# State space stage of a fused convolution and transformer kernel: decay held in PSUM and scanned in two halves, rows of B broadcast by DMA, convolution folded into a weight, preparation moved from VectorE

## The reference, cut to what matters

```python
xi, z = split(W_in @ xn)                      # 128 x 1024 each
xc = silu(conv_b + sum_k conv_w[:, k] * xi[:, t - 3 + k])      # 4 taps along the positions
dt, B, C = split(W_x @ xc)                    # 4, 16 and 16 rows of 1024
delta = softplus(W_dt @ dt + b_dt)            # 128 x 1024
for each position t and each state n:
    h[d, n] = h[d, n] * exp(-exp(A_log[d, n]) * delta[d, t]) + delta[d, t] * xc[d, t] * B[n, t]
    y[d, t] = sum_n h[d, n] * C[n, t]
out = W_out @ ((y + xc * Dp) * silu(z)) + x
```

## Time and profile before

| | us |
|---|---|
| median of 3 runs | 4073.43 (4072.83 to 4073.93) |
| the profiled execution, its time | 4079.2 |
| its span in the trace | 4077.5 |

### The profile page before, as it was taken

How to read it: one execution, slowest core, us unless ns; L and a number is a source line. 1 busy time by engine, 2 the same in 40 slices (tenths; PEclk the granted TensorE clock), 3 DMA queues, 4 the chain that set the end, 5 groups by cost and what they waited for, 6 DMA issues and landing times. The chain is left out here.

```text
span 4077.5 us, 56384 instructions
## 1 busy us (share of the span) xinstructions
PE 3426.7 (84%) x19376; PEld 1233.0 (30%) x19376; DVE 2982.9 (73%) x3235; ACT 2143.2 (53%) x2331; POOL 2103.6 (52%) x586
## 2 busy tenths in 40 slices
PE   6999999999999999999978996567777777767766
PEld 2333333333333333333322333222222222222222
DVE  5677677676776767767722221489999999999999
ACT  3566566565665656656543332255555554555554
POOL 0556556565565555655660000156665666656665
PEclk7999999999999999999998998778888888888888
DMA  2000000000000000000013111200000000000000
GB/s 93 11 14 17 10 14 17 15 14 14 10 17 15 14 15 12 14 15 14 12 39 111 67 36 54 102 9 8 9 12 8 10 8 8 13 8 10 8 8 8
DMA packets 34702, 90.68 MB, mean 22 GB/s; under 512 B 8304, under 2 KB 9396, under 8 KB 34356
## 3 DMA queue, kind: packets, MB, share of 16 engines
q1 hardware_dynamic: 29396, 70.53, 5.6%
q0 software_dynamic: 5056, 16.83, 1.1%
HBM read 49.03 MB, written 38.27 MB: 21 GB/s over the span
## 5 line engine op out<-in xcount | busy, mean ns | idle before, releaser
L526 DVE TENSOR_REDUCE at_pmax<-at_ring 128x1 f32<-128x512 f32 x2048 | 1305.1, 685 | 511.4 <-PE at_ring L334 510.8
L479 ACT ACTIVATE at_probs<-at_sc 128x1024 f32<-128x1024 f32 x1024 | 992.5, 1021 | 659.6 <-PE at_sc L401 659.5
L1623 POOL TENSOR_TENSOR ss_drive<-ss_du,ss_bsb 128x1024 f32<-128x1024 f32 x261 | 865.2, 3333 | 392.4 <-ACT ss_bsb L1469 312.9
L580 POOL TENSOR_TENSOR at_prob_sums<-at_prob_sums,at_probs 128x2048 f32<-128x2048 f32 x192 | 869.4, 4528 | 109.8 <-ACT at_probs L479 98.7
L398 PE MATMUL at_sc<-at_QT,at_KT 32*128 32x512 f32 x4096 | 848.2, 643 | 21.3 <-issue 20.9
L1560 DVE TENSOR_TENSOR_SCAN ss_state<-ss_decay,ss_drive 128x1024 f32<-128x1024 f32 x259 | 774.7, 2991 | 7.5 <-ACT ss_decay L1476 5.1
L580 POOL TENSOR_TENSOR at_prob_sums<-at_probs 128x2048 f32<-128x2048 f32 x64 | 291.0, 4547 | 789.9 <-ACT at_probs L479 789.9
L1377 PE MATMUL ss_Y<-ss_seen,ss_ident 128*128 128x512 f32 x1032 | 598.3, 710 | 58.7 <-DVE ss_yv L1577 58.7
L410 PE MATMUL at_O<-at_probs,at_V 128*32 128x512 f32 x4096 | 538.9, 610 | 53.0 <-DVE at_att L549 51.8
L1469 ACT ACTIVATE ss_bsb<-ss_B 128x1024 f32<-128x1024 f32 x262 | 268.3, 1024 | 537.1 <-PE ss_B L1359 535.9
L334 PE MATMUL at_ring<-at_KH,at_QH 32*128 32x512 bf16 x2048 | 447.3, 389 | 5.7 <-DVE at_pmax L526 2.9
(11 more groups left out here) (192 smaller groups left out, 2846.2 us busy)
## 6 DMA issues: line engine op xcount, KB each, us to landing
scratch_attn<-at_att SPq DMA_DIRECT2D x64, 256.0 KB, 2.0
fc_att<-scratch_attn SPq DMA_DIRECT2D x32, 512.0 KB, 5.8
at_xn<-scratch_xn SPq DMA_DIRECT2D x32, 256.0 KB, 3.8
ss_xn<-scratch_xm SPq DMA_DIRECT2D x17, 256.0 KB, 3.5
ss_xw<-scratch_xw SPq DMA_DIRECT2D x17, 256.0 KB, 3.4
ln_x<-in_x SPq DMA_DIRECT2D x8, 512.0 KB, 4.8
scratch_xn<-ln_xn POOLq DMA_DIRECT2D x8, 512.0 KB, 3.0
fc_x<-in_x SPq DMA_DIRECT2D x8, 512.0 KB, 7.7
```

The costliest lines, as they stand in the source:

```text
L479: nc.scalar.activation(probs[:, kb, two, :].rearrange("p h q -> p (h q)"), sc[:, two, :].rearrange("p h q -> p (h q)"), ACT.Exp, scale=SCA ...
L526: nc.vector.tensor_reduce(pmax[:, quad // 2, h, quad % 2:quad % 2 + 1], ring[:, unit[3], :], AX_X, ALU.max, negate=True).then_inc(max_done, 1)
L580: nc.gpsimd.tensor_tensor(prob_sums[:, half, :, :], before, probs[:, k, :, :], ALU.add).then_inc(pool_sums, 1)
L1623: nc.gpsimd.tensor_tensor(drive[:, n % DEPTH, :], du[:, par, :], bsb[:, n % DEPTH, :], ALU.mult).then_inc(drive_done, 1)
```

## The change

- `decay` becomes a PSUM tile in place of `Bp`, single, in two halves of 512 positions that lie in different banks. ScalarE makes 32 half tiles an image instead of 16 whole ones, one state ahead; VectorE runs two scans a state, the second beginning with the first one's last column.
- The rows of B: ScalarE copies them once an image from `aux` to `brow`, SyncE writes them to memory (`write_rows`, 16 rows of 4 KB) and reads each back into all 128 partitions (`spread_b`), into eight buffers `bsb`, six states ahead. TensorE's 16 spreads of B and ScalarE's 16 copies are gone.
- The convolution: at the start TensorE and ScalarE make `w_taps`, W_in multiplied by each tap's diagonal. `xn` is loaded twice, the second copy one position further, so that two matmuls with 128 contracted rows do four taps. VectorE's four operations and the `xpad` copy are gone; ScalarE makes `pre` with the bias.
- VectorE loses the high part (now ScalarE), the low part and `delta` (now GpSimd), `xc * Dp` (now a diagonal matmul into `Y`) and the addition of x (now an identity matmul, and ScalarE copies the sum in state 2). It keeps the scans, the product with C, the rest, and one product with the gate.
- Softplus: Abs and Relu both read `aux` directly with the bias.
- SyncE now goes state by state. `load_x` of the next image stands at state 3, behind `between`, which stores the image before once `res_done` says that it is there.

The core of the diff, with all that the prediction speaks of:

```diff
-        xn = sb("ss_xn", [P, S])
+        w_taps = sb("ss_w_taps", [P, 2, DI])
+        diag = sb("ss_diag", [P, KC + 1, P])
+        xn = sb("ss_xn", [P, S + KC - 1])
-        decay = sb("ss_decay", [P, DEPTH, S])
-        bsb = sb("ss_bsb", [P, DEPTH, S])
+        brow = sb("ss_brow", [N, 2, S])
+        bsb = sb("ss_bsb", [P, SLOTS, S])
-        aux, Bp, Cp, Y = ps("ss_aux"), ps("ss_B"), ps("ss_C"), ps("ss_Y")
+        aux, decay, Cp, Y = ps("ss_aux"), ps("ss_decay"), ps("ss_C"), ps("ss_Y")
...
         def _(sp):
+            def load_x(b):
+                load(xn[0:C, KC - 1:], xn_d, b, xn_in)
+                load(xn[C:P, KC - 2:KC - 2 + S], xn_d, b, xn_in)
...
+            def write_rows(b, par):
+                sp.wait_ge(brow_done, b + 1)
+                sp.dma_start(rows_d[par], brow[:, par, :]).then_inc(rows_out, DMA)
+
+            def spread_b(b, par, n):
+                if n == 0:
+                    sp.wait_ge(rows_out, (b + 2) * DMA)
...
+                    sp.wait_ge(drive_done, b * N + n - SLOTS + 1 + DEPTH)
+                sp.dma_start(bsb[:, n % SLOTS, :], rows_d[par, n:n + 1, :].broadcast_to([P, S])).then_inc(b_in[n % SLOTS], DMA)
+
+            def step(b, par, n):
+                if n == AT_REST:
+                    write_rows(b + 1, 1 - par)
+                spread_b(*ahead(b, par, n, B_LEAD))
+                if n == TURN:
+                    sp.wait_ge(gate_done, b + 1)
+                    load_x(b + 1)
+
+            def between(b, par):
+                store(b)
                 load(xw[:, 1 - par, :], xw_d, b + 1, xw_in)
...
+                    for now in loop_steps(2 * j + g, g):
+                        step(*now)
+                    between(2 * j + g, g)
...
         def _(pe):
-            pe.wait_ge(cleared, 3)
+            pe.wait_ge(consts_in, 11 * DMA)
...
+            for k in range(KC):
+                m = nc.tensor.matmul(Cp[0:C, k * DI:(k + 1) * DI], w_plain[:], diag[:, k, :], start=True, stop=True)
...
                     for h in range(2):
-                        m = nc.tensor.matmul(aux[:, hs(h)], w_in[:, 0:DI], xn[:, hs(h)], start=True, stop=True)
+                        for k in range(KC // 2):
+                            m = nc.tensor.matmul(aux[:, hs(h)], w_taps[:, k, :], xn[:, h * HALF + 2 * k:(h + 1) * HALF + 2 * k],
+                                                 start=(k == 0), stop=(k == KC // 2 - 1))
...
                 if n == 0:
-                    pe.wait_ge(y_step, 2 * b + 1)
+                    pe.wait_ge(y_step, b + 1)
+                    for h in range(2):
+                        nc.tensor.matmul(Y[:, hs(h)], diag[:, KC, :], u_in[:, par, hs(h)], start=True, stop=False)
...
             def step(b, par, n):
-                spread_b(*ahead(b, par, n, LEAD + 1))
-
+                if n == 0:
+                    pe.wait_ge(low_done, b + 1)
                 pe.wait_ge(seen_done, b * N + n + 1)
...
                             for h in range(2):
-                                m = nc.tensor.matmul(aux[0:C, hs(h)], w_out[:], yv[1][:, hs(h)], start=True, stop=True)
+                                nc.tensor.matmul(aux[0:C, hs(h)], w_out[:], yv[:, hs(h)], start=True, stop=False)
+                                m = nc.tensor.matmul(aux[0:C, hs(h)], ident[0:C, 0:C], xw[:, g, hs(h)], start=False, stop=True)
                             m.then_inc(out_ready, 1)
...
         def _(act):
+            def take_out(b):
+                act.wait_ge(out_ready, b + 1)
+                act.wait_ge(stored, (b + 1) * DMA)
+                nc.scalar.activation(res[:], aux[0:C, :], ACT.Copy).then_inc(res_done, 1)
...
-                act.wait_ge(state_done, b * N + n + 1)
-                nc.scalar.activation(decay[:, n % DEPTH, :], delta[:, par, :], ACT.Exp, scale=a_neg[:, n:n + 1])\
-                    .then_inc(decay_done, 1)
+                for h in range(2):
+                    if not (isinstance(b, int) and b == 0 and n == 0):
+                        if h == 0:
+                            act.wait_ge(first_half_done, b * N + n)
+                        else:
+                            act.wait_ge(state_done, b * N + n + DEPTH)
+                    nc.scalar.activation(decay[:, hs(h)], delta[:, par, hs(h)], ACT.Exp, scale=a_neg[:, n:n + 1])\
+                        .then_inc(decay_done, 1)
...
-                copy_b(*ahead(b, par, n, LEAD + 1))
-                make_decay(*ahead(b, par, n, LEAD))
+                make_decay(*ahead(b, par, n, 1))
+                if n == 2 and not isinstance(b, int):
+                    take_out(b - 1)
...
         def _(dve):
-                nc.vector.tensor_tensor_scan(state[:, n % 2, :], decay[:, n % DEPTH, :], drive[:, n % DEPTH, :], 0.0,
+                now = state[:, n % 2, :]
+                dve.wait_ge(decay_done, 2 * (b * N + n) + 1)
+                nc.vector.tensor_tensor_scan(now[:, hs(0)], decay[:, hs(0)], drive[:, n % DEPTH, hs(0)], 0.0,
+                                             ALU.mult, ALU.add).then_inc(first_half_done, 1)
+                dve.wait_ge(first_half_done, b * N + n + 1)
+                dve.wait_ge(decay_done, 2 * (b * N + n) + 2)
+                nc.vector.tensor_tensor_scan(now[:, hs(1)], decay[:, hs(1)], drive[:, n % DEPTH, hs(1)], now[:, HALF - 1:HALF],
                                              ALU.mult, ALU.add).then_inc(state_done, 1)
...
-                    nc.vector.tensor_tensor(yv[1][:], yv[0][:], gate[:, par, :], ALU.mult).then_inc(y_step, 1)
+                    nc.vector.tensor_tensor(yv[:], gate[:, par, :], Y[:], ALU.mult).then_inc(y_step, 1)
...
         def _(pool):
+            def low(b, par):
+                pool.wait_ge(mid_done, 2 * b + 2)
+                nc.gpsimd.tensor_tensor(bc[4 * N:6 * N, par, :], bc_rest[:], bc_mid[:], ALU.subtract).then_inc(low_done, 1)
...
             def make_du(b, par):
+                pool.wait_ge(soft_done, b + 1)
+                pool.wait_ge(relu_done, b + 1)
+                nc.gpsimd.tensor_tensor(delta[:, par, :], lin[:], soft[1][:], ALU.add).then_inc(delta_done, 1)
```

More of the change, by code:

```diff
@@ L1218, in state_space_phase @@
     DEPTH = 4
-    assert N % DEPTH == 0
+    SLOTS = 8
+    B_LEAD = 6
+    assert N % DEPTH == 0 and N % SLOTS == 0
     with ExitStack() as ctx:
@@ L1302, in store @@
                 sp.dma_start(out_d[bass.ds(b, 1)].rearrange("a c s -> (a c) s"), res[:]).then_inc(stored, DMA)
-            def image(b, par):
-                sp.wait_ge(gate_done, b + 1)
-                load(xn[0:C, :], xn_d, b + 1, xn_in)
-                if not isinstance(b, int) or b:
-                    store(b - 1)
-                    sp.wait_ge(stored, b * DMA)
-                    sp.sem_inc(res_free, 1)
+            def write_rows(b, par):
+                sp.wait_ge(brow_done, b + 1)
+                sp.dma_start(rows_d[par], brow[:, par, :]).then_inc(rows_out, DMA)
@@ L1313, in image @@
+            def step(b, par, n):
[7 more added lines that the diff above has]
+                store(b)
                 load(xw[:, 1 - par, :], xw_d, b + 1, xw_in)
             load(xw[:, 0, :], xw_d, 0, xw_in)
-            for b in range(2):
-                image(b, b)
@@ L1318, in _ @@
-            with sp.Fori(1, NB // 2) as j:
+            write_rows(0, 0)
+            for n in range(B_LEAD):
+                spread_b(0, 0, n)
+            for n in range(TURN):
+                step(0, 0, n)
+            with sp.Fori(0, NB // 2) as j:
                 for g in range(2):
-                    image(2 * j + g, g)
-            store(NB - 1)
-            sp.wait_ge(stored, NB * DMA)
+                    for now in loop_steps(2 * j + g, g):
+                        step(*now)
+                    between(2 * j + g, g)
@@ L1387, in step @@
                         unit(b + 1, 1 - par, k)
-            for k in range(2):
+            for k in range(4):
                 unit(0, 0, k)
-            pe.wait_ge(consts_in, 11 * DMA)
-            for k in range(2, 4):
-                unit(0, 0, k)
-            for n in range(LEAD + 1):
-                spread_b(0, 0, n)
             for n in range(TURN):
@@ L1447, in softplus @@
                     act.wait_ge(delta_done, b)
[L1448 to L1450 removed]
+                nc.scalar.activation(soft[0][:], aux[:], ACT.Abs, bias=cols[:, 1:2]).then_inc(abs_done, 1)
+                nc.scalar.activation(lin[:], aux[:], ACT.Relu, bias=cols[:, 1:2]).then_inc(relu_done, 1)
                 act.wait_ge(abs_done, b + 1)
@@ L1491, in step @@
                     softplus(b + 1)
-            for n in range(LEAD + 1):
-                copy_b(0, 0, n)
-            for n in range(LEAD):
-                make_decay(0, 0, n)
+            make_decay(0, 0, 0)
             for n in range(TURN):
@@ L1631, in step @@
                 make_drive(*ahead(b, par, n, LEAD))
+            low(0, 0)
             make_du(0, 0)
@@ L1642, in _ @@
                         step(*now)
+                        if now[2] == AT_LOW:
```

(2 more changed lines are left out.)

167 lines of the change are left out of this document (73 added, 94 removed).

## The result

| | before | after |
|---|---|---|
| median, us | 4073.68 (4 runs beside it) | 3974.12 (3961.56 to 3979.77, 4 runs) |
| profiled execution | 4079.2 | 3973.87 |
| its span | 4077.5 | 3972.2 |

The ratio is 0.9751 (95% interval 0.9727 to 0.9774). The change takes 100 us off where 212 were forecast: the sign held, and the time lies in the range of 3780 to 4000, but only in the part that was there for rival (b); the forecast proper, 3820 to 3925, was missed. In the later comparisons the kernel before had a median of 4078.2 (11 runs), 4078.5 (9 runs) and 4075.9 (7 runs), so a difference of 5 us between runs of two comparisons says nothing.

What follows compares the result with a forecast made beforehand. It took VectorE and GpSimd in alternation as the bound; a period of 61.3 + 2.4 + 1.5 + 7.2 = 72.4 us instead of 86.1, with the ends, took 212 off for a median of 3862; range 3780 to 4000.

Steps and rivals of the forecast that it cites:

- (b): More handshakes end late than counted (GpSimd's chain, landings slowed by rows of B, or both): 3925 to 3990 us; chance 0.20.
- the forecast proper: Whole kernel: period 70 to 76 us an image, time 3820 to 3925 us; chance 0.50.
- The scans: VectorE, every state: half scans from PSUM escape the exclusion with GpSimd, at 1.22 and 1.27 us; every drive 2.35.
- The list: VectorE's own work per image: 16 states of 3.69 us, the rest and the gate product, 61.3 us in all.
- The wait at state 4: VectorE waits for TensorE's spread of C, behind the late load of x: 7.2 us an image, bounds 4.7 to 10.7.
- The wait at state 2: VectorE waits for C, spread by TensorE only after four groups of 1.71 us: 1.5 us an image.
- The waits of states 8 to 14: ScalarE's insertions at states 8 and 12 delay the single decay: stalls of 1.3 and 1.1 us, 2.4 an image.
- Ends: Outside first scan to last gate product: start +17 us (8 to 25), end -3.
- (a): The load of x is not late: period 66 us an image, time 3760 us; chance 0.13.
- (c): VectorE's scan still excludes GpSimd's drive: 4040 to 4110 us, near no change; chance 0.04.
- (d): Rows of B, all DMA engines reading the same 4 KB, bound the kernel: 4610 us at a quarter rate; chance 0.13.

Runs made afterwards that it cites:

- e1: Changed kernel with the loads of x issued five states ahead, in state 10, instead of in state 3 behind the store: 3804.54 us.
- e2: Changed kernel with the loads of x issued just ahead of the store of the image before, instead of behind it: 3804.46 us.
- e3: Changed kernel with decay as a single SBUF tile instead of PSUM, still in two halves: 4198.13 us.
- e12: Changed kernel with x five states ahead, output and x products in halves at separate states, and e10's eight filler products: 3755.01 us.
- e9: Changed kernel with 24 bfloat16 filler products on TensorE while it waits for x to land: 3957.53 us.
- e7: Changed kernel with rows of B sent to 16 of 128 partitions from image 1 on (output differs): 3999.33 us.
- e10: e1 with eight filler products in TensorE's idle stretch at the end of state 11: 3799.68 us.

## Why the prediction was wrong in size and right in mechanism

*The step that failed* is the size of VectorE's waits, in the sum 61.3 + 2.4 + 1.5 + 7.2. The forecast had 7.2 at state 4 and 1.5 at state 2 for TensorE's spread of C and 2.4 at states 8 to 14 for ScalarE, 11.1 in all; measured are 16.5, and the wait at state 4 is the largest part of the difference. That the waits at states 2 and 4 would come, and the chain behind them, was right; most of the wait at states 8 to 14 has another cause than the one forecast.

*The scans.* Right. 1.216 and 1.282 against 1.22 and 1.27, drives at 2.35, and without the decay in PSUM the exclusion comes back (4198 and 4103 us). The rate of the Trainium skill (VectorE: DVE Perf Modes, The TRN2 errata) for a source in PSUM, 62 cycles more, does not show: an operation of 1024 columns takes 1.221 with one (the product with C) and 1.218 without (`delta`), and the half scan came out at its price without the addition.

*The list.* 61.3 forecast, 62.9 found. A state takes 3.80 from start to start (3319.57 to 3323.37 in the trace), not 3.69: 0.12 lies between the end of the first half scan and the start of the second, where I took 0.03. The second waits for the first by semaphore, but so does the product with C for the scan before it, and that starts 0.04 behind, so why it is 0.12 stays open. 16 x 0.1 = 1.6.

*The wait at state 4.* This is the term that was mis-sized: 10.3 measured, 7.2 forecast, and within its bounds (4.7 to 10.7) near the worse end. Counted from the end of the gate product (3319.65 in the timeline), link by link: the result is copied at 8.9 (8.3 forecast); the last load is issued at 12.4 (10.45), since the five issues from the store on take 3.5 and not 2.2; it lands at 17.4 (14.65), after 5.0 and not 4.2; C for state 4 is there at 26.2 (22.35), since seven of the eight records of the product are slow, not four. Each link is 0.6 to 1.4 longer, 3.8 together; VectorE wanted it 0.9 later than forecast. The first image and e1 show the term's whole worth, e2 its cause.

*The wait at state 2.* 2.6 in the mean, 1.5 forecast. At the full clock it is 2.12, since the four groups ahead of the spread take 7.6 (3319.80 to 3327.41) and not 4 x 1.71; and it is 3.82 in the quarter of the images in which TensorE is at the half clock, which I had not put there.

*The waits of states 8 to 14.* 3.6 against 2.4. The forecast put them down to ScalarE. That is right only for the 1.0 at state 10 of five images. In the other ten it is C at states 9 and 10, and at state 13 it is C, behind two groups of 3.78 at the half clock where it waits longest.

*Sum.* 1.6 + 3.1 + 1.1 + 1.2 = 7.0 us an image, which is 79.4 less 72.4; 15 images make 105 us of the 112 by which the median misses 3862. Nearly all the rest is that the median of after equals its profiled execution (3974.12, 3973.87), where I put it 5.8 lower.

*Ends.* In the profiled executions the phase starts 4.4 later after (2644.12 against 2639.73), by phases that are not touched. From there to the first scan are 50.6 us against 39.2: 11.4 more where I had 17; 3.2 of that is that making the taps and the first product with x take less (4.5 and 6.4, not 6.5 and 7.6). From the last gate product to the end 16.6 as before, where I had 3 less: the two groups ahead of the last image's output product meet the half clock (3.31 and 2.26, where an image inside the phase, at 3319.80 and 3321.59, has 1.96 and 1.88), which makes 1.7 of it. First scan to last gate product is 1260.8 instead of 1382.0. 15.8 - 121.2 + 0 = -105.4, which is the difference of the two profiled times. That the ends come to 15.8 where I had 14 is luck: 5.6 too much at the start stand against the 3 at the end and the 4.4 ahead of the phase.

*The rivals.* (a), a load of x that is not late, came out at 3804 in e1 and not at 3760: a period of 68.3 instead of 66, of which the list makes 1.6, and three longer images at the start. (b) is the nearest to what happened: 3925 to 3990 with late handshakes worth 4 to 8 us an image more than counted; they were worth 5.4 more, and the list 1.6. Of its two causes the rows of B slow the load of x by 1.0, and the chain of GpSimd is waited for once, before the first scan. (c) is refuted for a decay in PSUM. With the decay in SBUF it holds, and e3 came out above its 4040 to 4110 because the waits at states 2 and 4 (11.8 us an image there) are paid on top, not covered as (c) had it in part. (d) is refuted: the drives of after wait for VectorE, never for the rows. 8.4 MB of rows in 79.4 us are 106 GB/s, and in the 64.9 us of e12 129 GB/s; the windows, with all other traffic, show 125 and 152. Its sum is also off by a little: 4073 + 16 x 34 is 4617, not 4610. And in the earlier trace rows slice 27, in which the first image starts, shows 8; the 9s begin with slice 28. Neither bears on the outcome.

*Left open.* Which records of TensorE fall on the half clock. A long wait ahead brings it (e9 took it off the product with x by filling the wait), but records after no idle time over 2.6 us have it too, and in e7, e9 and e10 it moved to another state when one gap was filled or shortened. No run here settles what puts it where it is.

## What to carry to other kernels

Before moving a load to just ahead of its use, follow the queue that issues it back to the last wait in front of it: the store of the previous result had the next input wait for it, and one line of order was worth 170 us where the whole change gave 100. When the engine that bound the kernel is freed, write the next one's list as pieces between two of its deadlines: the same products in halves gave 28 us, where moving one of them whole to a later state lost 17. An operand moved to PSUM takes VectorE out of the way of GpSimd: with it the change gave 100 us, and nine operations off VectorE's list without it gave none. What either is worth by itself was not run.

## What the hardware showed that I had not expected

- TensorE's clock turns a short wait into a long one. With x late the granted clock of the window is 0.85, with x early 0.95, and the same product costs 6.1 to 6.6 or 3.60; some 40 of the 170 us (an estimate, 15 times 2.5 to 3.0) are the clock, not the load.
- It can also take a gain back. Loads that land 1.0 us sooner (e7) made the kernel 25 us slower, since 14 images of 15 instead of 4 had the half clock at state 2 (3.82 against 2.12 of wait), and again 14 instead of 4 had the 3.1 at state 13.
- The half clock comes after short gaps too: four records in 3.78 after 2.41 idle. The row behind 3.68 of idle in the earlier trace rows made me look for it in one place only.
- 24 products that compute nothing, put into a wait, speed up the work behind it (6.62 to 3.70 in twelve images, to 5.40 in three); the time did not fall beyond its uncertainty.
- One 4 KB row read by 128 partitions at once (512 KB) lands in 6.8 us, with 125 GB/s moved in all and no drive waiting. What it costs here is the 1.0 us by which the load of x beside it lands later.
